# Second normalisation and feed-forward layer of six batches moved into the loop over head pairs; output weights scaled in pieces

## What is computed

```python
# attention, on the layer norm of x
scores = q @ k * SCALE + q @ rel_k                  # per head
scores = where(scores < 32nd largest of the row, -inf, scores)
attn = softmax(scores)
v_curr, res = v, 0
for i in range(3):
    v_curr = attn @ v_curr (+ attn @ rel_v for i == 0)
    res += sigmoid(alphas_raw[i]) * v_curr
x = x + res @ Wout.T + bout
# feed-forward, on the layer norm of the new x
result = n @ base_w.T + base_b
gating = softmax(n @ router_w.T + router_b)         # 8 experts, rounded to bf16
lora = einsum(n @ lora_A, lora_B, gating)           # rank 8
x = x + result + 2 * lora
```

## Time and profile before

| | us |
|---|---|
| median of 3 runs | 726.46 (726.28 to 728.13) |
| profiled execution: its time | 727.17 |
| its span, first to last instruction | 725.4 |
| last `top` of the loop ends | about 685.1 |

### The profile page before, as it was taken

How to read it: one execution, slowest core, us unless ns; L and a number is a source line. 1 busy time by engine, 2 the same in 40 slices (tenths; PEclk the granted TensorE clock), 3 DMA queues, 4 the chain that set the end, 5 groups by cost and what they waited for, 6 DMA issues and landing times.

```text
span 725.4 us, 20794 instructions
## 1 busy us (share of the span) xinstructions
PE 656.9 (91%) x5736; PEld 511.6 (71%) x5736; DVE 684.4 (94%) x2841; ACT 619.4 (85%) x1754; POOL 535.1 (74%) x917
## 2 busy tenths in 40 slices
PE   4377989999999999999999999999999999998795
PEld 3255777777777777777777777777777777776574
DVE  5898989999999999999999999999999999999825
ACT  3668788989999899999999899999999899997843
POOL 1588888878887778878887778878887778777511
PEclk9779999999999999999999999999999999999998
DMA  6735444444545454554545454444545454453202
GB/s 196 191 108 147 132 121 146 136 146 137 150 138 152 125 160 129 153 150 133 149 132 151 131 161 139 143 146 137 149 132 157 127 159 140 143 149 110 63 21 59
DMA packets 148338, 98.72 MB, mean 136 GB/s; under 512 B 10624, under 2 KB 147968, under 8 KB 148096
## 3 DMA queue, kind: packets, MB, share of 16 engines
q1 hardware_dynamic: 147920, 97.32, 46.1%
q10 hardware_dynamic: 304, 0.08, 0.0%
HBM read 45.59 MB, written 51.77 MB: 134 GB/s over the span
## 4 chain that ended last, share of the span: by engine, by line
DVE 74%; issue 10%; POOL 6%; PE 5%; DMA 2%; ACT 2%; SPq 0%; ACTq 0%; POOLq 0%; DVEq 0%
DVE top L668 38%; DVE work L674 33%; POOL s_sb L322 3%; DMA band_scratch<-zeros 1%; DVE rinv L655 1%; POOL s_sb L297 1%; PE ps_p L888 1%; ACT a_sb L437 1%; POOL wk L365 1%; POOL x_sb L370 1%; PE ps_s L966 1%; PE ps_y L903 1%; PE ps_d L874 1%; ACT pen L427 1%; DVE stats L691 0%
## 5 line engine op out<-in xcount | busy, mean ns | idle before, releaser
L668 DVE MAX8 top<-work 128x8 f32<-128x256 f32 x768 | 285.3, 414 | 0.0
L674 DVE MATCH_REPLACE8 work<-top,work 128x256 f32<-128x256 f32 x512 | 206.4, 412 | 0.0
L322 POOL TENSOR_TENSOR s_sb<-s_sb,pen 128x512 f32<-128x512 f32 x127 | 162.0, 1276 | 59.6 <-ACT pen L427 59.6
L327 POOL TENSOR_SCALAR a_sb<-a_sb,rinv 128x256 f32<-128x256 f32 x254 | 119.3, 481 | 57.2 <-DVE rinv L655 56.6
L437 ACT ACTIVATE a_sb<-s_sb,nmax 128x256 f32<-128x256 f32 x256 | 128.1, 501 | 34.9 <-POOL s_sb L322 26.9
L427 ACT ACTIVATE pen<-s_sb,limit 128x256 f32<-128x256 f32 x254 | 116.4, 511 | 34.7 <-POOL limit L309 34.7
L297 POOL TENSOR_TENSOR s_sb<-s_sb,skew 128x384 f32<-128x384 f32 x128 | 128.4, 1003 | 2.7 <-DMA skew<-band_scratch 2.7
L888 PE MATMUL ps_p<-aT,rows 128*64 128x256 f32 x1024 | 125.1, 385 | 4.9 <-issue 3.3
L674 DVE MATCH_REPLACE8 work<-top,s_sb 128x256 f32<-128x256 f32 x256 | 103.1, 412 | 0.0
L888 PEld LDWEIGHTS ps_p<-aT,rows 128*64 128x64 f32 x1024 | 70.1, 136 | 41.8 <-issue 16.1
L668 DVE MAX8 top<-s_sb 128x8 f32<-128x256 f32 x256 | 94.6, 412 | 4.1 <-POOL s_sb L297 4.1
(11 more groups left out here) (135 smaller groups left out, 1285.0 us busy)
## 6 DMA issues: line engine op xcount, KB each, us to landing
skew<-band_scratch SPq DMA_DIRECT2D x128, 192.0 KB, 2.7
diag_scratch<-a_sb SPq DMA_DIRECT2D x128, 192.0 KB, 2.4
band_scratch<-band SPq DMA_DIRECT2D x128, 191.0 KB, 3.5
diag<-diag_scratch SPq DMA_DIRECT2D x128, 128.0 KB, 2.3
wqkv<-in_wqkv SPq DMA_DIRECT2D x1, 1152.0 KB, 7.7
x_sb<-in_x SPq DMA_DIRECT2D x4, 256.0 KB, 4.9
wout<-in_wout SPq DMA_DIRECT2D x1, 512.0 KB, 5.4
out<-xn SPq DMA_DIRECT2D x1, 512.0 KB, 3.3
```

The lines of the kernel that those rows point to most:

```text
L322: nc.gpsimd.tensor_tensor(s_sb[g % 4][:], s_sb[g % 4][:], pen[g % 2][:], ALU.subtract).then_inc(pen_added, 1)
L327: nc.gpsimd.tensor_scalar(a_sb[g % 3][:, t, :], a_sb[g % 3][:, t, :], rinv[g % 2][:, t:t + 1], 1.0, ALU.mult, ALU.mult).then_inc(normed, 1)
L668: nc.vector.max(m[:, t, 8 * n:8 * n + 8], src).then_inc(top_step, 1)
L674: nc.vector.match_replace(work[t][:, n % 2, :], m[:, t, 8 * n:8 * n + 8], src, LOW).then_inc(top_step, 1)
```

## The change

- In slots 20, 28, ..., 60 (`layer_slot(q)` gives f = 0 to 5) PE does `second_columns(f)` behind `scores(q + 1)` and `layer(f)` behind `third_power(q - 4)`; ACT does `save_ynT(f)` before `save_scores` and `save_layer(f)` before `exponent(2q)`. Both use the PSUM bank `ps_y`. The bias of the layer comes from two more matmuls with the identity, so that ACT can save the result.
- POOL makes the reciprocal root itself (`second_scale`, a sum and a power, slots 13, 21, ..., 61), normalises (`second_normal`, slots 14, 22, ..., 62) and adds the base result (`add_base`, slots 23, 31, ...). ACT's Sqrt behind the start is gone.
- The output bias is put into `ps_y` by two matmuls per batch in `project`; `add_bout` is gone. `wk` is made in 24 pieces of 128x128, three in each of the slots 1 to 8.
- `values(q - 1)` and `save_values(q - 1)` stand first in slots 61 to 63, and those of pair 63 at the end of slot 63.
- Behind the loop only batches 6 and 7 are left for normalisation and layer; gates, middle and experts of batches 0 to 5 come earlier, among the last pairs' powers, and the output goes out as batches 0 to 3, 4 and 5, 6 and 7.

```diff
-        ps_x = [ps_s0, ps_s1, ps_s0, ps_s1, ps_y]
-        ps_f = [ps_s0, ps_s1, ps_s0, ps_s1, ps_s0, ps_s1, ps_s0, ps_p0]
+        ps_x = [ps_y] * (B - 2) + [ps_s0, ps_y]
+        ps_f = [ps_y] * (B - 2) + [ps_s1, ps_p0]
+        def layer_slot(q):
+
+            f = (q - NP - 4) // NP - 1
+            return f if q % NP == 4 and 0 <= f < INSIDE and q < PAIRS else None
-        DONE = TILES - T
+        INSIDE = B - 2
 ...
+            def scale_wout(hp, a, e):
+
+                pool.wait_ge(alpha_done, 1)
+                pool.wait_ge(wout_in, 16 * 2)
+                for i in range(a, e):
+                    nc.gpsimd.tensor_scalar(wk[:, i, hp, :], wout[:, hp, :], al[:, hp, i:i + 1], 1.0, ALU.mult,
+                                            ALU.mult).then_inc(wk_done, 1)
+
+            def second_scale(b):
+
+                i = slice(T * b, T * (b + 1))
+                pool.wait_ge(row_stats, 2 * TILES + 2 * T * (b + 1))
+                nc.gpsimd.tensor_scalar(rstd[:, i], mv[:, i, 1], EPS, 1.0, ALU.add, ALU.mult).then_inc(var2_done, 1)
+                pool.wait_ge(var2_done, b + 1)
+                nc.gpsimd.tensor_tensor(rstd[:, i], rstd[:, i], halves[:], ALU.pow).then_inc(rstd2_done, 1)
+
+            def second_normal(b):
+                pool.wait_ge(rstd2_done, b + 1)
+                for i in range(T * b, T * (b + 1)):
+                    nc.gpsimd.tensor_scalar(yn[:, i, :], y_sb[:, i, :], mv[:, i, 0:1], rstd[:, i:i + 1], ALU.subtract,
+                                            ALU.mult).then_inc(yn_done, 1)
+
+            def add_base(b):
+
+                i = slice(T * b, T * (b + 1))
+                pool.wait_ge(f_saved, b + 1)
+                nc.gpsimd.tensor_tensor(y_sb[:, i, :], y_sb[:, i, :], ffn[:, i, 0:DIM], ALU.add).then_inc(by_done, 1)
 ...
                     negative_max(2 * q + 1)
+                if 1 <= q <= NP:
+                    scale_wout(q - 1, 0, 2)
+                if q >= NP + 5 and q % NP == 5:
+                    second_scale(q // NP - 1)
+                if q >= NP + 6 and q % NP == 6:
+                    second_normal(q // NP - 1)
+                if q >= 2 * NP + 7 and q % NP == 7:
+                    add_base(q // NP - 2)
+                if on(q):
                     add_penalty(2 * q)
                 if on(q + 1):
                     add_skew(2 * q + 2)
+                if 1 <= q <= NP:
+                    scale_wout(q - 1, 2, ORDER)
                 if on(q):
                     normalise(2 * q)
 ...
+            def save_ynT(b):
+                act.wait_ge(ynT_ready, b + 1)
+                nc.scalar.copy(ynT[:, T * b * P:T * (b + 1) * P], ps_x[b][:, 0:T * P]).then_inc(ynT_saved, 1)
+
+            def save_layer(b):
+                act.wait_ge(f_ready, b + 1)
+                nc.scalar.copy(ffn[:, T * b:T * (b + 1), :].rearrange("p t c -> p (t c)"),
+                               ps_f[b][:, 0:T * FFN]).then_inc(f_saved, 1)
 ...
                     save_diagonals(q - 2)
+                if layer_slot(q) is not None:
+                    save_ynT(layer_slot(q))
                 if on(q + 1):
                     save_scores(q + 1)
 ...
                     save_first(q - 2)
+                if layer_slot(q) is not None:
+                    save_layer(layer_slot(q))
                 if on(q):
                     exponent(2 * q)
 ...
             def project(p):
                 b, hp = divmod(p, NP)
-                pe.wait_ge(wk_done, ORDER)
+                pe.wait_ge(wk_done, ORDER * min(p + 1, NP))
                 pe.wait_ge(r1_saved, 2 * p + 2)
                 pe.wait_ge(r2_saved, p + 1)
                 if hp == 0:
                     reach(pe, y_done, b)
+                    reach(pe, f_saved, b - 1)
+                    for t in range(T):
+                        mm(ps_y[:, t * DIM:(t + 1) * DIM], ident[:], bout[:], start=(t == 0), stop=False)
 ...
+            def second_columns(b):
+                pe.wait_ge(yn_done, T * (b + 1))
+                pe.wait_ge(y_done, b + 2 if b < INSIDE else b + 1)
+                for t in range(T):
+                    last = transpose(ps_x[b][:, t * P:(t + 1) * P], yn[:, T * b + t, :], ident[:])
+                last.then_inc(ynT_ready, 1)
+
+            def layer(b):
+
+                pe.wait_ge(ffn_in, 64)
+                pe.wait_ge(ynT_saved, b + 1)
+                for t in range(T):
+                    i = b * T + t
+                    if b < INSIDE:
+                        mm(ps_f[b][:, t * FFN:(t + 1) * FFN], ident[:], bffn[:], start=True, stop=False)
+                    last = mm(ps_f[b][:, t * FFN:(t + 1) * FFN], ynT[:, i * P:(i + 1) * P], wffn[:], start=(b >= INSIDE),
+                              stop=True)
+                last.then_inc(f_ready, 1)
 ...
                     scores(q + 1)
+                if layer_slot(q) is not None:
+                    second_columns(layer_slot(q))
                 if on(q - 1):
                     attention_columns(2 * q - 2)
 ...
                     third_power(q - 4)
+                if layer_slot(q) is not None:
+                    layer(layer_slot(q))
                 if on(q - 2):
                     first_power(q - 2)
```

More of the change, by code:

```diff
@@ L358, in slot @@
                     add_skew(2 * q + 2)
+                if 1 <= q <= NP:
+                    scale_wout(q - 1, 2, ORDER)
                 if on(q):
                     normalise(2 * q)
[L362 to L379, removed]
+            pool.wait_ge(made, MADE)
             for q in range(-3, PAIRS - 1):
                 slot(q)
[L383 to L386, removed]
             q = PAIRS - 1
@@ L398, in _ @@
             normalise(2 * q)
+            add_base(INSIDE - 1)
             clip_block(q - 1)
             clip_block(q)
-            for i, (a, e) in enumerate(((0, 4), (4, 8), (8, DONE), (DONE, TILES))):
-                add_base(i, a, e)
+            add_base(B - 2)
+            second_scale(B - 1)
+            add_base(B - 1)
         @block.scalar
@@ L529, in slot @@
                     save_aT(2 * q - 1)
+                if on(q - 1) and on(q + 3):
                     save_values(q - 1)
+                if q == PAIRS - 1:
+                    save_values(q)
                 if on(q - 2):
                     save_rows(q)
[L534 to L540, removed]
             def gate_weights(i, a, e):
@@ L594, in _ @@
             save_third(q - 1)
[L595 to L605, removed]
+            save_ynT(B - 1)
+            gate_weights(1, T * INSIDE, TILES)
+            save_zT(2, INSIDE, B)
         @block.vector
@@ L931, in slot @@
                     queries_and_keys(q + 3)
+                else:
+                    values(q - 1)
                 if on(q + 2):
@@ L947, in slot @@
                     attention_columns(2 * q - 1)
+                if on(q - 1) and on(q + 3):
                     values(q - 1)
+                if q == PAIRS - 1:
+                    values(q)
                 if on(q - 4):
@@ L952, in slot @@
                     powers_back(q)
-            def second_columns(g, a, e):
-                pe.wait_ge(yn_done, e)
-                reach(pe, ynT_saved, g - 1)
-                for i in range(a, e):
-                    last = transpose(ps_x[g][:, (i - a) * P:(i - a + 1) * P], yn[:, i, :], ident[:])
-                last.then_inc(ynT_ready, 1)
-            def layer(b):
-                pe.wait_ge(ynT_saved, 4 if b < B - 1 else 5)
-                reach(pe, f_saved, b - 1)
-                for t in range(T):
-                    i = b * T + t
-                    last = mm(ps_f[b][:, t * FFN:(t + 1) * FFN], ynT[:, i * P:(i + 1) * P], wffn[:], start=True, stop=True)
-                last.then_inc(f_ready, 1)
             def middle_columns(i, a, e):
                 pe.wait_ge(z_done, 1 if e < B else 2)
+                if i == 0:
+                    pe.wait_ge(v_saved, PAIRS)
+                if i == 1:
+                    pe.wait_ge(t_saved, HEADS)
                 for b in range(a, e):
```

99 lines of the change are left out of this document (38 added, 61 removed).

## The result

The changed kernel takes 749.41 us (median of 4 runs, 748.91 to 749.94) against 727.3 us: 1.0308 times as long, 95% interval 1.0295 to 1.0322. It is slower, as forecast, but by 22 us and not by 9; 749.4 us lies above the range of 729 to 744. The profiled execution's span is 748.2 us, where 734.3 us were forecast.

The account below looks back on a forecast made before the run. The prediction took VectorE's (DVE's) `top`, head after head, to bound the loop's middle. Span: 725.4 + 21.0 (layer slots) + 3.4 (clock) - 15.5 (gains) = 734.3 us; with the median 1.1 us above it, 735.4 us, range 729 to 744.

Parts of the forecast that it names:

- The wait and its way to DVE: Layer slots 20, 28, ..., 60: PE waits about 2.9 us for add_projection, delaying divide; 3.5 us a slot, 21.0 us.
- The echo of 0.5 us: Behind each layer slot: late save_rows and ramp cost DVE another 0.5 us, then 0.1 to 0.2 us.
- The clock: Layer slots: PE's standstill lowers the granted clock in two of six, 1.7 us each; 3.4 us (0 to 10.2).
- the clock falls in all six: Rival, layer slots: the clock falls in every one, 10.2 us and not 3.4, giving 742.2 us; chance 0.13.
- POOL's small steps: Slots 5 to 7 of eight: second_scale, second_normal and add_base hide in POOL's 0.83 us gap; cost 0.
- The start: Start of the loop: removing big POOL pieces (scale_wout, add_bout) ends late divides; gain 8.9 us.
- The tail: Behind the last top: less PE work gains 3.2 us and a shorter last batch 1.8 us.
- The last batch: Tail: chain to second_normal falls from 4.83 to 2.05 us, four tiles cost 1.0 us more; net gain 1.8 us.
- The powers' part: Tail, PE part: transposes, layers and values(63) go, middle transposes and expert tiles come; gain 3.2 us with waits.
- PE catches up: Rival, layer slots: PE runs work behind the wait closer together, 1.5 us lost a slot, 720.3 us; chance 0.08.
- The power is dear: Rival, POOL's second_scale: a power of 1.28 us costs 4.6 us over seven slots, 740.0 us; chance 0.06.

Follow-up runs that it names:

- the spread steps: Changed kernel with GpSimd's small steps spread over five slots, the power a step of its own, batch 6 as it was: 745.87 us.
- the two products: Changed kernel with the subtraction in GpSimd's second_normal replaced by a product, so rows of batches 0 to 6 are not normalised: 745.73 us in one execution.
- the mended version: Changed kernel with add_projection before top(2q), GpSimd's small steps spread, later wk pieces, bias at the fourth pair, idle tail matmuls: 717.15 us, ratio 0.9854.

## Why the forecast was right in its direction and wrong in its size

**The wait and its way to DVE: right, step for step.** For slot 20 the forecast had transposes 0.07 us behind the addition, PE's stop of 2.9 us, `first_power` 4.19 us late, `divide` 2.95 us. Measured in slot 28, where the clock stayed, are 0.15 us, 2.89 us, 4.41 us and 3.17 us (3.08 idle). The 0.22 us between 4.19 and 4.41 are all of the difference: 0.09 us lie in front of `attention_columns`, and `layer` takes 1.17 us and not 1.09. The echo of 0.5 us and the later 0.1 to 0.2 us are 0.50 and 0.19. With 3.86 us a slot in place of 3.5 the term was 2.2 us too small; 4.0 was its bound. The experiments with the wait alone and with the wait gone show both halves of it.

**The clock: right mechanism, size by guess.** Two falls were taken, three came in the profiled run, one of them of 2.9 us. Among the profiled runs with this wait five of six, six of six and five of six slots fell (the wait alone, the spread steps, the two products) and none with the wait filled. One gap of 2.95 us in the trace before with a fall behind it was good evidence for "likely"; two of six was on the low side. Over the four profiled runs with the wait open 19 of 24 slots fell, which is nearer to the rival "the clock falls in all six"; that it was three in the changed kernel's, with 6.2 us between 3.4 and 10.2, was chance.

The price of 1.7 us a fall was right for two of the three, 1.63 and 1.62 us. The first cost more than the one row could say: 2.93 us, with 6.2 us at half rate and not 3.4. A price read from one case should have had a wider bound.

**POOL's small steps: this step failed.** The forecast put them at nothing: `second_normal` at 0.65 us for two pieces, hidden in 0.83 us. It had no row for a piece with a subtraction and took the price from other kinds. Two pieces took 1.58 us: 0.66 us late in seven periods, 4.6 us, and 0.19 us of `second_scale` once. The bound for this step came only from the power (722 ns, inside its bounds of 0.15 and 1.28 us, and hidden nearly everywhere). No bound was put on the subtraction. The trace before holds no POOL instruction that subtracts a per-partition value; the earlier trace rows could only say how long other kinds take. What was open was treated as known.

**The start: nearly right.** -8.2 and not -8.9 us. The idle places that the forecast lists sum to 8.4 us. It left out the 0.18 us echoes of the old delays (1.3 us more to gain) and the new delays of 2.2 us that come in the first slots; that the two nearly cancel is luck. The pieces are not their cause: in the mended version, where the pieces come two slots later, heads 3 and 4 are late as well (steps of 5.58 and 6.06 us). They go with the clock of the start. In the changed kernel's trace it is back at 46.9 us and head 4 is 1.46 us late, in the mended one's at 45.6 and 1.02, with the steps spread at 45.1 and 0.82; with the early addition it is back at 39.1, and neither head 3 nor head 4 is late. No run was made to try this by itself, and a few other late `divide`s before slot 12 come and go between the profiled runs.

**The tail: this step failed too.** 5.0 us were forecast and 1.6 us came, in two halves.
- The last batch was to give 1.8 us and gave nothing (14.2 us from the last `project` to the end before, 14.3 after). The chain in front of `second_normal` came near the forecast, though the power took 0.5 us more than assumed: 2.3 us in place of 4.83, a gain of 2.5 and not 2.8 us. What stands behind it grew by 2.6 us, from 9.4 to 11.9, where the forecast had 1.0. PE, now idle for 2.98 us, works on at the half clock:

```profile
736.92 0.69 PE L948 MATMUL ps_y<-ident,xn 128*128 128x128 f32 x2 [2.98 <-DVE xn L735]
...
738.16 1.30 PE L959 MATMUL ps_p<-wffn,xnT 128*128 128x144 f32 x4 [0.55 <-ACT xnT L530]
```

 With PE kept busy (the filled wait) these take 0.44 and 0.73 us, and what stands behind `second_normal` takes 10.4 us: 1.0 more than before, as forecast. So the missing 1.6 us are the clock, which the forecast counted for the layer slots and forgot here. Before, PE had transposes and experts of batches 0 to 6 in this place, was idle for 1.48 us in front of the transposes, and its clock fell only behind the last gap, at 720.9.
- The powers' part was to give 3.2 us and gave 1.6. The work taken away in front of `attention_columns(127)` (`values(63)`, 0.45 us) gained nothing, because that step now waits for DVE's `normalise_last`:

```profile
713.89 0.66 PE L815 MATMUL ps_a<-ident,a_sb 128*128 128x128 f32 x4 [0.74 <-DVE a_sb L729]
```

 It comes 5.24 us behind the last `divide` in the loop (that of head 126), and came 5.21 us behind it before, without a wait: there DVE's result was ready 4.85 us behind that `divide`, and now it is after 5.18. From there to the end of the last `project` it was 21.7 us and is 20.1. The removed transposes had filled waits for ACT's saves (0.38 us of idle time now stands before `powers_back` at 716.97). How the rest divides was read from the trace and not tried.

**The rivals.** "PE catches up" (720.3 us) is out: `attention_columns` was 3.19 us late in slot 28, `layer` took 1.17, and `first_power` was 4.41 us late. From `attention_columns` to `first_power` it was 2.80 us before and is 4.02 us with `layer` in between, so nothing was won back. The rule of the Trainium skill in "Trainium Kernel Development and Optimization", Best Practices, to judge the distance to roofline by MFU (the share of its peak rate that TensorE reaches) and the weight loads' share and not by matmul busy time, did not foretell this: the weight loads show 75% in the middle before, and still even the early addition, with no wait in the layer slots, made `divide` late by 0.31, 0.50 and 0.20 us there. What decided was what stands in front of `first_power` in PE's queue. "The power is dear" had the right engine and the wrong instruction; that its 4.6 us are the 4.6 us of `second_normal` is luck.

The range ended at 744 us because it added one rival at a time to the sum. Three terms (layer slots +2.2, clock +2.8, POOL +4.8) and the tail's +3.4 all went the same way. The first two stayed within their bounds. POOL's and the tail's did not: the gains came to 11.6 us, where 13 to 17 were forecast. Without these two misses the time would have been 749.4 - 4.8 - 3.4 = 741.2 us (an estimate), inside the range.

## What to carry to other kernels

When a step is put into a slot that an engine works through in order, look first at what it waits for and when the producer's own order gives it; here the bank that two uses shared made PE wait 2.9 us for an addition that DVE's order had put behind a search of 5 us, and moving that addition in front of the search, with no work less, was worth 23 us of 749. A wait of nearly 3 us in a full TensorE queue can be paid twice, since the clock may fall behind it. And an instruction whose kind the trace doesn't show (here a subtraction and a product with per-partition values in one GpSimd instruction) needs a bound of its own; here it took twice its nearest relative, 789 and 373 ns.

## What the runs showed of the hardware that was not expected

- On GpSimd a 128x128 `tensor_scalar` of two products takes 373 ns with one per-partition operand and 445 ns with two, but 789 ns with a subtraction and a product. A subtraction of one tile from another takes as long as a sum (1276 and 1272 ns for 128x512). A power with 2 elements a partition takes 722 ns, where a sum or product of that size takes 191.
- Behind idle times of 2.8 to 2.9 us of PE in an otherwise full loop the granted clock fell to 1.2 GHz in 19 of 24 cases and stayed at 2.4 GHz in the others; twelve matmuls nobody needs, put into the wait, kept it up in all six. A fall cost DVE 1.4 to 1.7 us in 17 of the 19, and 2.9 us in two.
